# A 39-tile expert FFN on one core: weight and p traffic reordered, idle products, DMA transposition from tile 7, experts read by twos, another end

## The reference

```
ys = cond * 256**-0.5
d  = rsqrt((ys*ys) @ (W*W) + 1e-8)
y  = ((x * ys) @ W) * d
lang = softmax(y @ lang_w.T + lang_b)               # 4 languages
logits = y @ router_w.T + router_b + 0.1*(pairs of lang)
p, e = top 2 of softmax(logits), p divided by its sum
out = x + sum over the two: p * (gelu(y @ w1[e] + b1[e]) @ w2[e] + b2[e])
```

## Time and profile before

| what | value |
|---|---|
| time, median of 3 | 298.06 us |
| the profiled execution's own time | 296.99 us |
| its span | 295.2 us |
| PE busy | 269.6 us (91%) |
| PE weight loads | 221.2 us (75%) |
| ACT, DVE, POOL busy | 195.2, 191.9, 175.4 us |
| DMA moved | 39.53 MB, mean 134 GB/s |
| chain that ended last | PE 73%, DVE 9%, issue 6%, DMA 5%, POOL 4% |

### The profile page before, as it was taken

One profiled execution on the slowest core, in us unless ns is written; L12 is line 12 of the kernel. 1 busy time (PEld: TensorE's weight loads), 2 busy tenths in 40 slices (PEclk: granted clock), 3 DMA queues, 4 the chain that ended last, 5 costly groups with the idle time before them and its releaser, 6 DMA issues.

```text
span 295.2 us, 8972 instructions
## 1 busy us (share of the span) xinstructions
PE 269.6 (91%) x3065; PEld 221.2 (75%) x3065; DVE 191.9 (65%) x430; ACT 195.2 (66%) x425; POOL 175.4 (59%) x160
## 2 busy tenths in 40 slices
PE   7899967899999999999999999999999989999800
PEld 5778957788799998877778777777777767877500
DVE  2957787799999897656655655555656555556510
ACT  3355469499897997677667676766776756776500
POOL 8200026833366989887777877767787657464340
PEclk9799996999999999999999999999999999999985
DMA  6799995499862234645535555534535434332220
GB/s 160 290 400 388 368 323 155 129 404 450 294 191 41 38 59 69 95 76 88 93 56 91 75 93 73 79 68 76 90 59 80 88 56 74 53 39 25 32 35 1
DMA packets 39881, 39.53 MB, mean 134 GB/s; under 512 B 19920, under 2 KB 35744, under 8 KB 39680
## 3 DMA queue, kind: packets, MB, share of 16 engines
q1 hardware_dynamic: 32320, 28.56, 31.7%
q0 software_dynamic: 7488, 10.39, 21.9%
q10 hardware_dynamic: 32, 0.01, 0.0%
HBM read 27.61 MB, written 9.64 MB: 126 GB/s over the span
## 4 chain that ended last, share of the span: by engine, by line
PE 73%; DVE 9%; issue 6%; DMA 5%; POOL 4%; ACT 0%; DVEq 0%; POOLq 0%
PE ps L639 30%; PE ps L656 28%; DVE wsp L940 5%; PE ps L537 5%; DMA out<-onehot,idx 4%; PE ps L555 3%; POOL out L468 2%; PE ps L648 1%; POOL onehot L459 1%; PE ps L479 1%; PE ps L615 1%; DMA rows<-y_rows,idx 1%; PE ps L510 1%; PE ps L519 1%; DVE dv L871 1%
## 5 line engine op out<-in xcount | busy, mean ns | idle before, releaser
L639 PEld LDWEIGHTS ps<-onehot,wsp 128*128 (+1 forms) x1872 | 130.0, 98 | 37.4 <-issue 2.9
L639 PE MATMUL ps<-onehot,wsp 128*128 128x128 f16 x1872 | 154.4, 219 | 1.8 <-issue 1.5
L818 ACT ACTIVATE pay<-ps,cur 128x128 f32<-128x128 f32 x312 | 117.5, 463 | 54.9 <-issue 39.9
L656 PE MATMUL ps<-wsp,pay 128*128 (+1 forms) x616 | 139.4, 316 | 1.2 <-DVE pay L1102 1.2
L468 POOL DMA_INDIRECT out<-onehot,idx x39 | 68.7, 1762 | 28.9 <-POOL onehot L459 12.1
L1102 DVE SCALAR_TENSOR_TENSOR pay<-pay,cur 128x512 f16<-128x512 f32 x72 | 54.9, 762 | 28.8 <-ACT pay L806 26.6
L437 POOL DMA_INDIRECT rows<-y_rows,idx x39 | 49.4, 1266 | 22.4 <-issue 11.0
L459 POOL TENSOR_SCALAR onehot<-onehot,cur 128x256 f32<-128x256 f32 x37 | 43.0, 1161 | 25.6 <-DVE onehot L1120 21.6
L656 PEld LDWEIGHTS ps<-wsp,pay 128*128 128x128 f16 x616 | 45.3, 97 | 5.0 <-issue 1.6
L1096 DVE TENSOR_SCALAR pay<-pay,cur 128x512 f16<-128x512 f32 x36 | 19.4, 538 | 26.4 <-ACT pay L818 24.1
L806 ACT ACTIVATE pay<-pay,cur 128x512 f16<-128x512 f32 x36 | 26.0, 722 | 1.2
(11 more groups left out here) (177 smaller groups left out, 193.0 us busy)
## 6 DMA issues: line engine op xcount, KB each, us to landing
stage<-in_L_ffn_w SPq DMA_DIRECT2D x9, 1024.0 KB, 9.9
wsp<-in_L_ffn_w SPq DMA_DIRECT2D x7, 1024.0 KB, 11.8
y_rows<-pay SPq DMA_DIRECT2D x4, 512.0 KB, 9.4
wsp<-in_x SPq DMA_DIRECT2D x3, 512.0 KB, 8.1
b2bc<-in_L_ffn_b SPq DMA_DIRECT2D x1, 1024.0 KB, 9.4
rows<-y_rows,idx POOLq DMA_INDIRECT x39
out<-onehot,idx POOLq DMA_INDIRECT x39
wsp<-in_x SPq DMA_DIRECT2D x2, 256.0 KB, 5.8
```

The source lines that it names most:

```text
L639: last = mm(ps[:, HB + (2 * j + g) % RING, c * P:(c + 1) * P], wsp[:, bass.ds(e, 1), o:o + P].rearrange("p a f -> p (a f)"), xsp[:, j % RI ...
L656: last = mm(ps[:, OB + j % 2, 0:width], hsp[:, (2 * j + g) % NH, part, c, :], wsp[:, bass.ds(e, 1), o + w:o + w + width].rearrange("p a f ...
L818: last = a.activation(to, ps[:, HB + (2 * j + g) % RING, c * P:(c + 1) * P], ACT.Gelu, bias=cur[:, j % CURS, cc:cc + 1], scale=cur[:, j % ...
```

## The change

1. SP no longer writes the p columns; POOL does, right behind their making. Weight load 7 (w2 of expert 3) moves ahead of the wait for p, and the load of b2 moves ahead of the first gathers.
2. PE gets idle products: 5 ahead of the wait for `picked`, 4 behind `gram(2)`, and WARM is 10 instead of 6.
3. The first up half of tile 0 stands ahead of the transposition of tile 1.
4. TURNED is 7 instead of 10: tiles 7, 8 and 9 are transposed by DMA.
5. BATCH is 2 instead of 8.
6. `outb` has five places (OUTS) instead of three.
7. The last three tiles (36 to 38) use three products of 256 columns (WIDE ends at 35), so that DVE needs one instruction a tile; in loops 36 and 37 PE does the down half ahead of the up half instead of mixing them; DVE makes the rows of tiles 35 and 36 ahead of the split of the next tile's h, as it did for tile 37.

```diff
+WIDE = range(E, NT - 3)
+OUTS = 5
-WARM = 6
+WARM = 10
-TURNED = 10
+TURNED = 7
-EARLY = 8
-BATCH = 8
+BATCH = 2
@@ SP @@
-            sp.wait_ge(p_ready, 1)
-            for b in range(NB):
-                sp.dma_start(y_tiles[:, b, :, D:ROW], payv[:, b * TB:(b + 1) * TB, D:ROW]).then_inc(p_written, 16)
             load_weights(7)
+            sp.wait_ge(p_written, 16 * NB)
+            sp.dma_start(b2bc[:, :, :].rearrange("p e d -> p (e d)"),
+                         b2.rearrange("(a e) d -> a (e d)", a=1).broadcast_to([P, E * D])).then_inc(b2_in, 16)
             for j in range(RING):
                 sp.wait_ge(gathered[j], 16)
             load_weights(12)
-            sp.dma_start(b2bc[:, :, :].rearrange("p e d -> p (e d)"),
-                         b2.rearrange("(a e) d -> a (e d)", a=1).broadcast_to([P, E * D])).then_inc(b2_in, 16)
             load_weights(10)
@@ POOL @@
             g.tensor_tensor(pex, pex, over(pe1[:, 1, :], E), ALU.mult).then_inc(p_ready, 1)
+            pool.wait_ge(p_ready, 1)
+            for b in range(NB):
+                g.dma_start(y_tiles[:, b, :, D:ROW], payv[:, b * TB:(b + 1) * TB, D:ROW]).then_inc(p_written, 16)
             scale_early(1)
@@ PE @@
             sum_squares(0)
+            pe.wait_ge(lg_read, T)
+            keep_warm(5, 1, 512)
...
             gram(2)
+            keep_warm(4, 1, 512)
             sum_squares(2)
...
             gram(3)
-            for _ in range(WARM):
-                mm(ps[:, RB, :], ones[:, :], onehot[:, 0:512], start=True, stop=True)
+            keep_warm(WARM, 1, 512)
...
-                if j < EARLY:
+                if j not in WIDE:
                     steps = ((0, 0, D), (0, D, D), (1, 0, D))
...
             transpose_rows(0)
+            blocks((0, 0), None)
             transpose_rows(1)
-            blocks((0, 0), None)
             blocks((0, 1), None)
...
-                blocks((j + 1, 0) if j + 1 < NT else None, (j - 1, 1) if j else None)
+                if NT - 4 < j < NT - 1:
+                    blocks(None, (j - 1, 1))
+                    blocks((j + 1, 0), None)
+                else:
+                    blocks((j + 1, 0) if j + 1 < NT else None, (j - 1, 1) if j else None)
@@ DVE, rows_out @@
-                if j >= RING:
-                    dve.wait_ge(added, 16 * (j - RING + 1))
+                if j >= OUTS:
+                    dve.wait_ge(added, 16 * (j - OUTS + 1))
...
-                                       op0=ALU.mult, op1=ALU.add).then_inc(o_read if j < EARLY else o_sum, 1)
-                if j >= EARLY:
-                    dve.wait_ge(o_sum, j - EARLY + 1)
+                                       op0=ALU.mult, op1=ALU.add).then_inc(o_sum if j in WIDE else o_read, 1)
+                if j in WIDE:
+                    dve.wait_ge(o_sum, WIDE.index(j) + 1)
@@ DVE, loop @@
-                if j == NT - 1:
+                if j > NT - 4:
                     rows_out(j - 1)
...
-                if 0 < j < NT - 1:
+                if 0 < j <= NT - 4:
                     rows_out(j - 1)
```

More of the change, by code:

```diff
@@ L213, in adaln_moe @@
         xsp = onehot[:, 0:RING * 2 * D].rearrange("p (r s k n) -> p r s k n", r=RING, s=2, k=KD)
-        outb = onehot[:, RING * 2 * D:RING * 4 * D].bitcast(F32).rearrange("p (r n) -> p r n", r=RING)
+        outb = onehot[:, RING * 2 * D:(RING + OUTS) * 2 * D].bitcast(F32).rearrange("p (r n) -> p r n", r=OUTS)
         ps = ctx.enter_context(nc.psum_tensor("ps", [P, 8, 512], F32))
@@ L458, in _ @@
                     pool.wait_ge(o_read, j + 1)
-                    g.tensor_scalar(outb[:, j % RING, :], outb[:, j % RING, :], cur[:, j % CURS, C_P:NCUR], None,
+                    g.tensor_scalar(outb[:, j % OUTS, :], outb[:, j % OUTS, :], cur[:, j % CURS, C_P:NCUR], None,
                                     ALU.mult).then_inc(o_ready, 1)
@@ L468, in _ @@
                 g.indirect_dma_start(out=out, out_offset=bass.IndirectOffsetOnAxis(ap=idx[:, j:j + 1], axis=0),
-                                     in_=outb[:, j % RING, :], in_offset=None,
+                                     in_=outb[:, j % OUTS, :], in_offset=None,
                                      compute_op=ALU.add).then_inc(added, 16)
@@ L824, in weigh @@
             def weigh(j):
-                r = j % RING
+                r = j % OUTS
                 act.wait_ge(o_read, j + 1)
@@ L1105, in rows_out @@
             def rows_out(j):
-                r, e = j % RING, expert(j)
+                r, e = j % OUTS, expert(j)
                 if j == 0:
```

## The result

| kernel | runs | median us | ratio to before |
|---|---|---|---|
| before | 4 | 297.84 (297.35 to 298.10) | |
| changed | 4 | 302.06 (301.79, 301.98, 302.13, 304.60) | 1.0163, interval 1.0106 to 1.0219 |

The change made the kernel slower by 1.6% (4.2 us between the medians, 4.9 us by the ratio), where I had forecast 2 us less: wrong in sign, and outside the range. The profiled execution took 302.13 us, 5.14 us more than that of before (296.99 us).

What follows compares the result with a forecast made beforehand. PE was taken to bound the tiles, with a slow turn, three load holes and a tail as exceptions. Terms -1.4 - 0.83 + 1.5 - 1.2 = -1.9 us from 298.06 gave 296.0 us, range 294.6 to 297.8 us.

Steps and rivals of the forecast that it cites:

- Reading by twos: PE, every second tile: 14 loads at 0.29 us, 4.1 us, less 2.55 us saved: a loss of 1.5 us.
- a load on PE over 0.3 us long: Register loads on PE: a sign that the prediction is wrong; 0.15 to 0.25 us each was expected.
- The rival of the fixed price: PE, every second tile from 12 on: each load costs 0.7 us whatever its size, +7.2 us, 301.9 us; chance 0.12.
- The turn: From front to tiles: load 7 early, idle products and tile 0's order start PE's tiles sooner, 1.4 us of gain.
- `idx` is some 0.5 us earlier: Front, ahead of the first gather: if idle products keep the clock up, `idx` comes some 0.5 us sooner.
- rival three: Turn, 46 to 53 us: clock falls all the same, front gives nothing or loses 0.5 us; chance 0.17.
- Transpositions: PE, tiles 7, 8 and 9: three transpositions go to DMA, a gain of 0.83 us in sum.
- The end: Last additions to `out`: down half first and one DVE instruction put the last addition 1.2 us earlier.
- the last four additions are bound by their landings alone: POOL, tail: additions from tile 35 on wait only for landings, 4.8 us apart, the last 1.2 us earlier.
- nothing to 0.3 us: PE, tiles 36 to 38: three products for two; an address more per step costs nothing to 0.3 us.
- p on POOL, b2, five row places: POOL's p DMAs fit its gap, b2 moves ahead of the gathers, rows get five places: nothing gained or lost.
- The rival that POOL pays per piece: POOL, front: p DMAs cost by their pieces, +14 us instead of -1.4, about 311 us; chance 0.05.

Runs made afterwards that it cites:

- kernel with eights: The changed kernel with BATCH 8 instead of 2, so experts are read by eights again: 296.25 us median, ratio 0.9935 to before.
- fours in the static tiles: The changed kernel with PE's experts read four at a time ahead of the blocks of tiles 0 to 7: 294.13 us, ratio 0.9857 to before.
- third group: Experiments with reads of four values, beginning with the changed kernel with BATCH 4 instead of 2: 297.41 us, ratio 0.9961 to before.
- The kernel before with the early loads: The kernel before, only with PE's experts read by fours ahead of the blocks of tiles 0 to 7: 295.16 us, ratio 0.9893 to before.
- the pair with fours: The changed kernel with PE's experts read by fours ahead of tiles 0 to 7, with TURNED 7 against 10: 294.13 and 295.83 us.
- two kernels with five early loads: The changed kernel, PE's experts in five loads ahead of tiles 1, 2, 3, 5, 7, DVE by eights: 296.45 us; with the old end 297.06 us.

## Why the prediction was wrong, step by step

**Reading by twos: the step that failed.** I priced a load of two at 0.19 us and 0.1 us besides, 14 of them at 4.1 us, a net loss of 1.5 us. Measured: 0.54 and 0.14 us, 12 of them 8.1 us to tile 35, less the 2.56 us of the loads by eights (kernel with eights against that with fours in the static tiles, from tile 9 to 35), and 1.1 us more in the end, where the loads of tiles 36 and 38 stand (26.62 us from tile 35's mark to the last addition, 25.5 us without them). That is +6.6 us. The place and the mechanism were as I had put them: PE's queue hides nothing past tile 8, and each load costs its length and 0.1 us. What failed is the term "0.19 us for a load of two", which measured 0.54 us, and the sign that I had named for it, a load on PE over 0.3 us long, is there in all 16 loads of the changed kernel. I had two equal rows of eight values (597 and 605 ns) and one of seven (1072 ns), and took from the longer that length goes with values, when seven values being longer than eight should have said that it goes by something else. The reading that fits all runs is that of the third group: 0.3 us for each full group of four if the load begins at a multiple of four, 0.25 us for each other value (eight: 2 x 0.3; seven from place 32: 0.3 + 3 x 0.25 = 1.05 us; two: 0.5 us; eight from place 15: 8 x 0.245 us; 31 from place 8: 7 x 0.32 + 3 x 0.25 + 0.2 us for the first). It is a fit; why the lengths go so, no run shows, and no load of four or more began at a place that was neither a multiple of four nor one below it. The loads from place 15 and of 31 values were not in the profile of before; seven against eight was. What PE pays besides is nearly the same for every size: 25 loads of one value cost 0.40 us each between tiles 9 and 35, those of four 0.45 us, of two 0.68 us, of eight or seven 0.85 us, always the length and about 0.1 us.

The rival of the fixed price gave 301.9 us, and 302.06 us came. Its number was right by luck in part: it had 0.7 us a load, which is what was paid, but the length isn't fixed, as the loads of one value show. The shortest loads took 297 ns for one value and 328 ns for four. The Trainium skill, "DMA: Bandwidth & Descriptors", section "Latency and other measured facts", gives a floor of about 600 ns and says that the compiler unrolls by four to amortize it; the remedy agrees with these rows and the floor doesn't, and the measurement decides. The Trainium skill, "Runtime: NRT & Kernel Launch", section "Instruction fetch mechanics", gives about 200 ns a register for loads from HBM even in bulk; that is another source than the on-chip `te`, whose single values took 0.25 us each and groups of four 0.08 us a value.

**The turn: -1.4 forecast, -0.2 measured.** Counted from PE's first counting product, which the change doesn't touch, the tiles begin 15.21 us after it in before and 14.80 us in the changed kernel; DVE's scales of group 3 come at 18.28 and 18.06 us, tile 3 at 41.54 and 41.33 us. Even the 0.2 us isn't told from nothing: tile 3's mark comes 40.96 to 41.90 us behind the counting product in ten profiles of the new front and 41.31 to 41.88 us in four of the old. The first step that failed is "`idx` is some 0.5 us earlier": the first gather comes 9.98 to 10.20 us behind the counting product in all 14 profiles, old front or new, low clock or full. The clock still fell (rival three), and where it doesn't, the gain isn't there either. The kernel with eights had 1.00 from 46 to 53 us:

```profile
48.97 2.02 PE L557 MATMUL ps<-wsp 128*128 128x128 bf16 x32
50.83 2.33 PE L481 MATMUL ps<-ones 128*128 128x512 f16 x10
53.72 0.40 PE L635 MATMUL ps<-ident,rows 128*128 128x128 f16 x4 [0.56 <-DMA rows<-y_rows,idx]
54.69 1.50 PE L643 MATMUL ps<-onehot,wsp 128*128 128x128 f16 x24 [0.57 <-ACT onehot L810]
56.37 0.40 PE L635 MATMUL ps<-ident,rows 128*128 128x128 f16 x4 [0.18 <-DMA rows<-y_rows,idx]
```

`gram(3)` is short and ends at 51.0 us, but PE then waits for the first gather (0.56 us; issued at 50.63 us, it lands 3.1 us later and not 2.8), the copy (0.57 us) and the second gather (0.18 us): tiles at 14.06 us, scales at 17.69 us behind the counting product. The kernel before with the early loads, at a clock of 0.55 in that stretch, has its scales at 17.84 us. So the slow `gram(3)` bound before only narrowly: the gathers stand close behind it, 0.15 to 0.6 us. I had seen "the copy ends last" and still booked the whole distance of 1.4 us to the row of splits. And the 0.43 us that the changed profile was ahead at the counting product are not of the change, since eight profiles of the new front had it at 39.93 to 40.86 us. A reading of the earlier trace rows was off too: only one slice around 50 us has a low clock (6 tenths, 44 to 52 us), and a second one (7 tenths) lies at 7 to 15 us; no term hung on it.

**Transpositions: -0.83 forecast, -0.25 to -0.55 measured** (tiles 3 to 9: 0.25 us in the pair with fours, 0.24 us from before to the kernel with eights, 0.55 us from before to the changed one). Each of the three was real work of PE, but not every one stood where only PE was late.

**The end: -1.2 forecast, -0.25 measured** (25.73 to 25.86 us from tile 35's mark to the last addition in three kernels with the old end, 25.31 to 25.68 us in seven with the new end and no load in it). The step that failed is that with both delays gone the last four additions are bound by their landings alone. POOL in the kernel with eights:

```profile
264.25 1.59 POOL L470 DMA_INDIRECT out<-onehot,idx  x1 [0.28 <-POOL onehot L461]
...
268.85 1.59 POOL L470 DMA_INDIRECT out<-onehot,idx  x1 [1.14 <-DMA out<-onehot,idx]
...
273.43 1.59 POOL L470 DMA_INDIRECT out<-onehot,idx  x1 [0.49 <-POOL onehot L461]
278.93 1.79 POOL L470 DMA_INDIRECT out<-onehot,idx  x1 [3.91 <-ACT onehot L835]
283.57 1.55 POOL L470 DMA_INDIRECT out<-onehot,idx  x1 [2.85 <-DMA out<-onehot,idx]
```

The additions of tiles 35 and 36 follow at 4.60 and 4.58 us (4.8 forecast), and that of tile 36 stands 1.20 us earlier behind tile 35's mark than in before, as I had it. But that of tile 37 comes 5.50 us later, bound by its own row. Here is ACT's multiplication of that row, in before and in the kernel with eights:

```profile
278.20 0.51 ACT L827 ACTIVATE onehot<-onehot,cur 128x256 f32<-128x256 f32 x1 [1.26 <-DVE onehot L1120]
```

```profile
278.14 0.51 ACT L835 ACTIVATE onehot<-onehot,cur 128x256 f32<-128x256 f32 x1 [0.84 <-DVE onehot L1123]
```

That is 19.26 us and 20.08 us behind tile 35's mark: the row comes 0.8 us later than before. The reason is a term that I had at "nothing to 0.3 us", the third product and the parted halves on PE. From the first up step of tile 35 to the last of tile 38 PE takes 20.90 us in before and 22.08 us in the kernel with eights; in the two kernels with five early loads, which differ in the end alone, 20.91 and 22.06 us. A step in which up products alternate with the three down products takes 0.80 us there in the mean of six, one with two down products 0.66 to 0.68 us in before. So the end costs PE 1.2 us, and that uses up most of what the landings gain. How the 1.2 us is shared between the third product and the order of the halves, no run tells. I had checked tile 38's row and not tile 37's.

**p on POOL, b2, five row places: nothing, as forecast.** The rival that POOL pays per piece is out: 1.04 us a DMA.

The sum: -0.2 - 0.55 + 6.6 - 0.25 = +5.6 us; with the 0.43 us of the front's luck +5.2 us, and the profiles differ by 5.14 us. Had only the load term been right, the forecast would have been 298.06 - 1.4 - 0.83 + 6.6 - 1.2 = 301.2 us, and the three gains, booked at 3.4 us, brought 1.0 us. What stays open is how that 1.0 us is shared out in timed runs: the runs scatter by more than that, and no pair of kernels tells the turn's edits from each other.

## What to carry to other kernels

When one instruction's length is unknown, ask whether any simple law fits the rows that there are; seven values in 1072 ns beside eight in 597 ns fit neither law I weighed, and that alone was a reason to give the extreme more than 0.12. A load on an engine's queue costs nothing while the queue is ahead by more than its length and its whole length afterwards: put all such loads where addresses are constants, in groups of four that begin at a multiple of four, each shorter than the lead. And where three waits end within half a microsecond of each other, removing the last is worth the distance to the next, not to its own new time.

## What the runs showed of the hardware

- A register load from on-chip memory took 297 to 322 ns for one value, 532 to 550 for two (once 616), 777 to 1022 for three, 328 to 346 for four at a multiple of four (once 407), 593 to 607 for eight so placed, 1937 to 1997 for eight that begin at place 15, 23 or 31, 1067 and 1072 for seven, 3155 for 31, all on PE. The first load of a program took 0.2 to 0.3 us more (588 for one, 724 and 801 for two).
- PE's queue was ahead of PE by about 1.0 us in the tiles with constant addresses (0.99 us of the load at 94.9 us were hidden) and by nothing that could hide 0.3 us in those with computed ones, where a load cost PE its length and about 0.1 us. Of the 0.68 us of a load of two, 0.29 us in the mean showed as idle time; of the 0.4 us of a load of one or four, nothing did.
- The first gather came 9.98 to 10.20 us behind PE's first counting product in all 14 profiles.
- With ten idle products instead of six and nine more ahead of them, the granted clock of 46 to 53 us was 0.76 to 1.00 in ten profiles of the new front (1.00 in five); in four profiles of the old front it was 0.51 to 0.74. Without the profiles whose clock was low already from 10 to 20 us it was 0.76 to 1.00 in eight and 0.51 and 0.55 in two.
